# Routing of a graph and expert layer on one core: ScalarE normalises the rows, VectorE takes the low parts, every second block is turned by a transposing DMA

## The reference, cut to what matters

```python
xn = _layernorm(x, axis=-1)
x = x + _L0_gnn_ref(xn, src, dst, edge_weight, W, b) + _L0_mix_ref(xn[None], ...)[0]
x = x + _L0_ffn_ref(_layernorm(x, axis=-1)[None], Wg, bg, W1, b1, W2, b2)[0]
# in _L0_ffn_ref:
gate_scores = einsum('bsd,ed->bse', x, Wg) + bg
topk_scores, topk_idx = top_k(gate_scores, 2)
```

## Time and profile before

| what | value |
|---|---|
| median of 3 runs | 2040.22 us (2038.3 to 2041.55) |
| profiled execution, its own time | 2043.48 us |
| its span (first to last instruction) | 2041.8 us |
| mean granted TensorE clock | 0.945 |
| PE busy | 1662.7 us, 81% |
| DVE busy | 1579.0 us, 77% |
| ACT busy | 1379.6 us, 68% |
| POOL busy | 1247.3 us, 61% |
| DMA traffic | 232.75 MB, mean 114 GB/s |

### The profile page before, as it was taken

How to read it: one execution, slowest core, us unless ns; L and a number is a source line. 1 busy time by engine, 2 the same in 40 slices (tenths; PEclk the granted TensorE clock), 3 DMA queues, 4 the chain that set the end, 5 groups by cost and what they waited for, 6 DMA issues and landing times. The chain is left out here.

```text
span 2041.8 us, 50410 instructions
## 1 busy us (share of the span) xinstructions
PE 1662.7 (81%) x15119; PEld 1287.6 (63%) x15119; DVE 1579.0 (77%) x3370; ACT 1379.6 (68%) x3988; POOL 1247.3 (61%) x1226
## 2 busy tenths in 40 slices
PE   5777668888888788898886666562799999999998
PEld 3455557666666577777764344342677777777776
DVE  8899859898888899989998989887355555555554
ACT  7565458788887778888878878575455555555554
POOL 4357757777777777777777777650344444444443
PEclk7899979999999999999999999855899999999999
DMA  6122355555554544444433346461344444444442
GB/s 223 44 70 80 110 167 157 158 157 159 153 160 151 158 139 124 124 124 121 122 106 101 102 154 185 130 206 26 78 72 73 73 74 71 72 74 71 74 71 43
DMA packets 197501, 232.75 MB, mean 114 GB/s; under 512 B 89207, under 2 KB 154657, under 8 KB 197123
## 3 DMA queue, kind: packets, MB, share of 16 engines
q0 software_dynamic: 62816, 134.68, 25.8%
q1 hardware_dynamic: 128070, 88.47, 15.4%
q10 hardware_dynamic: 6364, 6.40, 0.9%
HBM read 172.28 MB, written 44.36 MB: 106 GB/s over the span
## 5 line engine op out<-in xcount | busy, mean ns | idle before, releaser
L1011 POOL DMA_INDIRECT misc<-z_d,consts x814 | 784.6, 964 | 265.0 <-issue 160.6
L1261 DVE SCALAR_TENSOR_TENSOR acc<-ps,consts,acc 128x512 f32 x814 | 609.2, 748 | 79.3 <-PE ps L1363 60.7
L1034 ACT ACTIVATE misc<-misc 128x256 f16<-128x256 f16 x872 | 391.2, 498 | 74.5 <-DVE misc L1128 69.0
L1891 ACT ACTIVATE misc<-ps,misc 128x128 f32<-128x128 f32 x840 | 240.2, 368 | 276.1 <-PE ps L1851 166.9
L1361 PE MATMUL ps<-misc 128*128 128x256 f16 x1088 | 298.1, 274 | 110.7 <-ACT misc L1034 35.6
L1939 POOL DMA_INDIRECT out<-misc,pos x105 | 166.4, 1585 | 295.5 <-ACT misc L1960 244.7
L1849 PE MATMUL ps<-acc,big 128*128 128x128 f16 x1680 | 328.3, 220 | 14.9 <-DMA acc<-acc 10.0
L1851 PE MATMUL ps<-acc,big 128*128 128x128 f16 x1680 | 330.0, 220 | 0.0
L1850 PE MATMUL ps<-acc,big 128*128 128x128 f16 x1680 | 327.9, 220 | 0.0
L1870 PE MATMUL ps<-big,rec 128*128 x840 | 320.5, 382 | 0.1
L1363 PE MATMUL ps<-misc 128*128 128x256 f16 x1088 | 298.8, 275 | 0.0
(11 more groups left out here) (348 smaller groups left out, 3657.8 us busy)
## 6 DMA issues: line engine op xcount, KB each, us to landing
big<-in_w2T SPq DMA_DIRECT2D x60, 256.0 KB, 2.7
misc<-z_d,consts POOLq DMA_INDIRECT x814
big<-xT_d SPq DMA_DIRECT2D x98, 128.0 KB
big<-in_w1T SPq DMA_DIRECT2D x32, 256.0 KB, 2.8
tok_d<-misc SPq DMA_DIRECT2D x50, 132.0 KB, 1.8
xT_d<-misc SPq DMA_DIRECT2D x49, 128.0 KB
z_d<-misc SPq DMA_DIRECT2D x49, 128.0 KB, 1.7
acc<-in_x SPq DMA_DIRECT2D x6, 896.0 KB
```

Of the source, the lines that this page charges most:

```text
L1011: e.indirect_dma_start(out=rows[n % RB], out_offset=None, in_=c.z_d, in_offset=bass.IndirectOffsetOnAxis(ap=idx[u][:, k:k + 1], axis=0)).t ...
L1034: e.activation(hot[n % HG][:, half, :], same[n % OG], ACT.Copy, scale=near[n // UG % 3][:, t % UG, 1 + half:2 + half]).then_inc(s_hot, 1)
L1261: e.scalar_tensor_tensor(out=rows_of, in0=out_ps[tile % BG], scalar=c.gain, in1=rows_of, op0=ALU.mult, op1=ALU.add).then_inc(s_add, 1)
L1891: l = e.activation(hidden[:, m, :], h_ps[u][:, m, :], ACT.Relu, bias=b1x[u][:, m:m + 1])
```

## The change

What VectorE, ScalarE and GpSimd did for each block is dealt out anew, and one half of the blocks take another way to `xT`:

- `norm` is on ScalarE: one activation (Identity, with a scale and a bias for each partition) writes `xn[i]` in f32, and a second one of the same form, which reads `c.acc3` once more, writes the high part in f16 to `tok[i]`. The bias is -mean times the inverse deviation, one more short operation for each group (`nbias`) on VectorE, behind the reciprocal.
- `lower`, the subtraction of the high part, is on VectorE. GpSimd has nothing left to do in this block but three tables of numbers at its start.
- Blocks with an odd number are turned by a transposing DMA from `tok[i]` to `xT[i]`, issued by SyncE ahead of that block's store. Even blocks are turned by TensorE and copied by ScalarE as before.
- There are four `xn` and four `xT` in place of three and two. `gate(i)` stands two blocks behind `turn` in place of one, and the short operations of `settle` and `invert` and ScalarE's square root stand at other blocks of the group.

```diff
-    XB, TB, GB, LIFT = 3, 6, 7, 2048.0
+    XB, XT, TB, GB, LIFT = 4, 4, 6, 7, 2048.0
+    nbias = more.take(NT)
...
             for i in range(NT):
                 e.wait_ge(s_lo, i + 1)
+                if i % 2 and i >= XT:
+                    e.wait_ge(s_gate, i - XT + 1)
+                if i % 2:
+                    e.dma_start_transpose(xT[i % XT], tok[i % TB][:, 0:2 * D]).then_inc(s_xt[i % XT], 16)
                 e.dma_start(c.tok_d[i * P:i * P + P, :], tok[i % TB].bitcast(F32)).then_inc(s_st[i % TB], 16)
...
-                v.add(e.reciprocal(rstd[:, part], std[:, part]))
-
-            def norm(i):
-                if i >= XB:
-                    e.wait_ge(s_lo, i - XB + 1)
-                e.tensor_scalar(xn[i % XB], c.acc3[:, i:i + 1, :], mean[:, i:i + 1], rstd[:, i:i + 1],
-                                ALU.subtract, ALU.mult).then_inc(s_xn, 1)
+                v.link(e.reciprocal(rstd[:, part], std[:, part]))
+                e.scalar_tensor_tensor(out=nbias[:, part], in0=mean[:, part], scalar=-1.0, in1=rstd[:, part],
+                                       op0=ALU.mult, op1=ALU.mult).then_inc(s_nb, 1)
+
+            def lower(i):
+                e.wait_ge(s_xn, i + 1)
+                e.wait_ge(s_hi, i + 1)
+                e.tensor_tensor(tok[i % TB][:, D:2 * D], xn[i % XB], tok[i % TB][:, 0:D], ALU.subtract).then_inc(s_lo, 1)
...
-            for i in range(NT):
-                e.wait_ge(s_hi, i + 1)
-                e.tensor_tensor(tok[i % TB][:, D:2 * D], xn[i % XB], tok[i % TB][:, 0:D], ALU.subtract).then_inc(s_lo, 1)
...
-                e.copy(tok[i % TB][:, 0:D], xn[i % XB]).then_inc(s_hi, 1)
+                e.activation(xn[i % XB], c.acc3[:, i, :], ACT.Identity, bias=nbias[:, i:i + 1],
+                             scale=rstd[:, i:i + 1]).then_inc(s_xn, 1)
...
+                e.activation(tok[i % TB][:, 0:D], c.acc3[:, i, :], ACT.Identity, bias=nbias[:, i:i + 1],
+                             scale=rstd[:, i:i + 1]).then_inc(s_hi, 1)
...
-                if i >= 2:
+                if i >= 2 and i % 2 == 0:
                     turned_copy(i - 2)
-                if i % GB == (GB - 1 if i < GB else 5) and i < NT - GB:
+                if i % GB == (GB - 1 if i < GB else 4) and i < NT - GB:
                     deviation(i // GB + 1)
...
-            for i in range(NT + 1):
-                if i < NT:
+            for i in range(NT + 2):
+                if i < NT and i % 2 == 0:
                     turn(i)
-                if i >= 1:
-                    gate(i - 1)
+                if i >= 2:
+                    gate(i - 2)
```

More of the change, by code:

```diff
@@ L1422, in route @@
     bg, ones = more.take(NE), more.take(P)
-    XB, TB, GB, LIFT = 3, 6, 7, 2048.0
-    xn = [misc.take(D) for _ in range(XB)]
-    xT = [matrix(misc.take(2 * D, F16), 2 * DH, P) for _ in range(2)]
+    XB, XT, TB, GB, LIFT = 4, 4, 6, 7, 2048.0
+    nbias = more.take(NT)
+    xn = [(misc if k == 0 else more).take(D) for k in range(XB)]
+    xT = [matrix(misc.take(2 * D, F16), 2 * DH, P) for _ in range(XT)]
     tok = [misc.take(ROW, F16) for _ in range(TB)]
@@ L1432, in route @@
     s_blank, s_acc, s_dump = map(S, ("blank", "acc", "dump"))
-    s_w, s_v, s_var, s_std, s_ones, s_xn, s_tr, s_xt, s_gate, s_hi, s_lo = map(S, (
-        "weights", "vector", "var", "std", "ones", "xn", "tr", "xt", "gate", "hi", "lo"))
+    s_w, s_v, s_var, s_std, s_ones, s_xn, s_nb, s_tr, s_copied, s_gate, s_hi, s_lo = map(S, (
+        "weights", "vector", "var", "std", "ones", "xn", "nbias", "tr", "copied", "gate", "hi", "lo"))
+    s_xt = {k: S(f"turned{k}") for k in range(1, XT, 2)}
+    tr_ps = [matrix(c.bank[4 + u][:, 0:D].bitcast(F16), 2 * DH, P) for u in range(2)]
     s_score, s_half, s_wh, s_wl = S("score"), S("half"), S("gate_hi"), S("gate_lo")
     s_st, s_acc0 = [S(f"store{k}") for k in range(TB)], S("acc_first")
-    tr_ps = [matrix(c.bank[4 + u][:, 0:D].bitcast(F16), 2 * DH, P) for u in range(2)]
     g_ps = [matrix(c.bank[u][:, 0:GB * 2 * NE], GB, 2 * NE) for u in range(2)]
@@ L1510, in _ @@
                 g, n = i // GB, i % GB
-                if n == 0:
-                    v.sync()
-                norm(i)
                 if g < NT // GB - 1:
-                    at = n - 1 if g else n - 3
+                    at = n if g else n - 2
                     if 0 <= at < 4:
                         settle(g + 1, at)
-                    if n == GB - 1:
+                    if n == (5 if g else 6):
                         invert(g + 1)
@@ L1524, in _ @@
                         measure(AHEAD + k)
+                lower(i)
             score(NT // GB - 1)
@@ L1548, in rows_out, with norm @@
                             c.acc3[:, g * GB:g * GB + full, :]).then_inc(s_acc0 if g < 3 else s_acc, 16)
-            def high(i):
-                e.wait_ge(s_xn, i + 1)
+            def norm(i):
+                if i % GB == 0:
+                    e.wait_ge(s_nb, i // GB + 1)
+                if i >= XB:
+                    e.wait_ge(s_lo, i - XB + 1)
+                e.activation(xn[i % XB], c.acc3[:, i, :], ACT.Identity, bias=nbias[:, i:i + 1],
+                             scale=rstd[:, i:i + 1]).then_inc(s_xn, 1)
                 if i >= TB:
                     e.wait_ge(s_st[i % TB], 16 * (i // TB))
-                    e.wait_ge(s_tr, i - TB + 1)
-                e.copy(tok[i % TB][:, 0:D], xn[i % XB]).then_inc(s_hi, 1)
+                    if i % 2:
+                        e.wait_ge(s_xt[(i - TB) % XT], 16 * ((i - TB) // XT + 1))
+                    else:
+                        e.wait_ge(s_tr, (i - TB) // 2 + 1)
+                e.activation(tok[i % TB][:, 0:D], c.acc3[:, i, :], ACT.Identity, bias=nbias[:, i:i + 1],
+                             scale=rstd[:, i:i + 1]).then_inc(s_hi, 1)
             def turned_copy(i):
-                e.wait_ge(s_tr, i + 1)
-                if i >= 2:
-                    e.wait_ge(s_gate, i - 1)
-                e.copy(xT[i % 2], tr_ps[i % 2]).then_inc(s_xt, 1)
+                e.wait_ge(s_tr, i // 2 + 1)
+                if i >= XT:
+                    e.wait_ge(s_gate, i - XT + 1)
+                e.copy(xT[i % XT], tr_ps[i // 2 % 2]).then_inc(s_copied, 1)
             EARLY = 4
@@ L1565, in _ @@
             deviation(0)
-            for i in range(NT + 2):
+            for i in range(NT + 3):
                 if i < NT:
-                    high(i)
-                if i >= 2:
+                    norm(i)
+                if i >= 2 and i % 2 == 0:
                     turned_copy(i - 2)
-                if i % GB == (GB - 1 if i < GB else 5) and i < NT - GB:
+                if i % GB == (GB - 1 if i < GB else 4) and i < NT - GB:
                     deviation(i // GB + 1)
@@ L1582, in turn @@
                 e.wait_ge(s_lo, i + 1)
-                if i >= 2:
-                    e.wait_ge(s_xt, i - 1)
+                if i >= 4:
+                    e.wait_ge(s_copied, i // 2 - 1)
                 for h in range(2 * DH):
-                    l = e.transpose(tr_ps[i % 2][:, h, :], tok[i % TB][:, h * P:h * P + P], c.ident16)
+                    l = e.transpose(tr_ps[i // 2 % 2][:, h, :], tok[i % TB][:, h * P:h * P + P], c.ident16)
                 l.then_inc(s_tr, 1)
@@ L1590, in gate @@
                 g, n = i // GB, i % GB
-                e.wait_ge(s_xt, i + 1)
+                if i % 2:
+                    e.wait_ge(s_xt[i % XT], 16 * (i // XT + 1))
+                else:
+                    e.wait_ge(s_copied, i // 2 + 1)
                 if n == 0 and g >= 2:
@@ L1595, in gate @@
                 for h in range(DH):
-                    e.matmul(o, xT[i % 2][:, h, :], wg16[:, h, :], start=h == 0, stop=False)
+                    e.matmul(o, xT[i % XT][:, h, :], wg16[:, h, :], start=h == 0, stop=False)
                 for h in range(DH):
-                    l = e.matmul(o[:, 0:NE], xT[i % 2][:, DH + h, :], wg16[:, h, 0:NE], start=False, stop=h == DH - 1)
+                    l = e.matmul(o[:, 0:NE], xT[i % XT][:, DH + h, :], wg16[:, h, 0:NE], start=False, stop=h == DH - 1)
                 l.then_inc(s_gate, 1)
```

## The result

The changed kernel takes 2055.28 us (median of 5 runs, 2050.47 to 2057.07) against 2040.83 us (5 runs) for the kernel before; the ratio is 1.0066, 95% interval 1.0055 to 1.0077. The medians lie 14.5 us apart where 8.7 were forecast. The direction was right and 2055.3 lies 0.7 us inside the upper end of the range, but outside the 2046 to 2052 us of the forecast's own case: the size was too small.

The account below looks back on a forecast made before the run. VectorE, with ScalarE close behind, was taken to bound most of `route`'s first block. Afterwards ScalarE would bind: +8.2 us to the last copy and 0.5 for the transposing DMA, together +8.7, median 2048.9 us; range 2045 to 2056.

Parts of the forecast that it names:

- the forecast's own case: First block of `route`: ScalarE bound at 0.49 us an activation, transposes hidden; 2046 to 2052 us, chance 0.70.
- What bounds the block, and that it goes into the total in full: First block of `route`: VectorE bounds most of its loop, ScalarE close behind; its gain or loss reaches the total in full.
- The block ends with ScalarE's issues behind the last copy: End of `route`'s first block: ScalarE's last copy plus 4.6 us of DMA issues, which stay.
- ScalarE's price: ScalarE in the loop: 0.49 us an activation, 2.44 us a pair of blocks; last copy 8.2 us later.
- VectorE after: VectorE in the loop: without normalisation but with `lower`, 1.02 us a block at most, below ScalarE's 1.22.
- The transposing DMA: Odd blocks: SyncE's queue keeps up and transposes land within the cover; DMA traffic costs 0.5 us, bounds 0 and 1.0.
- The cover of 4.2 us: Odd blocks: time left for a transpose before ScalarE's copy is held up; it takes 2.65 us, leaving 1.55 us.
- the transpose comes late: Odd blocks: landing doubles to 5.3 us, 2.80 us a pair, +8.6 us on the 8.2, total 2057.0; chance 0.16.
- The signs of being wrong: In the loop: activations under 0.45 us, ScalarE waiting for `lower` in most blocks, or gates waiting for transposes and ScalarE behind.
- The cheap f16 activation: ScalarE's high part: f16 activation as cheap as the cast, 0.31 us; 8.8 us less, 2040.1, no change; chance 0.07.
- the faster case: Loop: VectorE's contention goes and ScalarE doesn't bind; 1.02 us or less a block, 2036.8; chance 0.04.

Follow-up runs that it names:

- with the cast and without the transposes: The change with the high part as a cast of the normalised rows and VectorE copying odd blocks, no transposing DMA: ratio 1.0000, stretch 54.1 us.

## Why the prediction was right, and where it was too small

- *What bounds the block, and that it goes into the total in full*: right. 664.0 to 665.9 us from the next block to the end in every kernel.
- *The block ends with ScalarE's issues behind the last copy*: right, shown by taking three of them out (3.0 and 3.5 us). In the change itself they take 3.76 + 1.51 us against 3.02 + 1.55, 0.7 us that the sum lacked; SyncE was still issuing three stores at that time, which may be why, but no run shows it by itself.
- *ScalarE's price*: right. 591 and 598 ns an activation, start to start 0.49; the kernel without transposes has a stretch of 61.7 us where 1380.3 - 1318.8 = 61.5 were worked out. The f16 output costs nothing and saves nothing. Of the forecast's 8.2 us 0.25 are a later first normalisation (0.2 measured, from the block's first DMA) and 7.9 are stretch, of which that kernel has 8.1.
- *VectorE after*: right that it has room, at most 5.30 of 7 us busy in the windows above.
- *The transposing DMA, forecast at 0.5 us between bounds of 0 and 1.0*: this term was mis-sized. It measured 5.4 us in the stretch. The step that failed is "a pair of blocks costs 1.19 + 2 x 0.32 = 1.83 us of SyncE against 2.44 of the pace", and from it that the queue keeps up. The store's 0.32 us was read where no transpose stood in the queue; two behind one take 1.05 together. A pair costs 2.40 us. Against a pace of 2.44 nothing was left, and each output DMA, behind which a transpose's issue takes 0.8 to 1.4 us longer, puts the queue behind for several pairs. The cover of 4.2 us was reckoned from the issue to the landing, as if the issue came at once; it was the issue that was late. The forecast's landing time of 2.65 us was right (median 2.5).
- *The rival "the transpose comes late"* had the right place and 0.16. Its mechanism, a landing of 5.3 us for all, was only part of it: 7 of the 24 landed 4.1 to 5.0 us after their issue began, most of them because the issue itself was long. Its time, 2057, was nearer the measured 2055.3 than the forecast was. The Trainium skill, "VectorE: DVE Perf Modes", section "The three transpose paths", has 1309 ns a tile; taken four times, the estimate of 5.2 us, it did not hold here either, since four tiles in one DMA land in 2.5 us (median).
- *The signs of being wrong*: one of them came true. TensorE's gates waited for the transposes, 46.1 us in all and over 1 us eleven times from 1350 us on, and ScalarE waited behind them. The last copy started at 1383.2 and the next block at 1389.2 us in an execution whose part in front was 2.65 us shorter, so at 1385.9 and 1391.8 by the prediction's clock. The signs named 1380.5 and 1385.6; by the prediction's own +8.7 they should have been 1380.8 and 1386.0.
- *The cheap f16 activation and the faster case*: out, by 591 ns. But some of the room that the faster case saw was there: with the cast and without the transposes the time is that of before, not less.

What stays open: how the 5.4 us divide between the queue's lateness and slower landings in the bursts. The runs show both (issues of 2.6 us; landings of up to 5.0 us), but taking the output DMAs away, which wins 3.9 us back, removes both at once. So the range held and the direction, for the larger part by ScalarE's price; that a term of 0.5 us where 5.4 were measured did not carry the time out of the range is luck.

## What to carry to other kernels

Price a queue by the rows of the mixture that will stand in it: the issue of a store in a queue of stores says little of one behind a transpose. Add up every engine and every queue per block, not only the one that binds first; here ScalarE (2.44 us a pair) and SyncE's queue (2.40) lay so close that easing ScalarE alone won 0.8 us, and easing both 13.0. And before work is taken off a busy engine, ask what the helper really saves: GpSimd's 33.8 us of subtractions were worth 0.6 us.

## What the runs showed of the hardware

- A store's issue on SyncE's queue takes 0.32 us in a queue of stores; two behind a transposing DMA take 1.05 us together. The transpose's own issue takes 1.20 us, and in the change 2.0 to 2.6 us where ScalarE's queue has just been given an output DMA of 896 KB; in the kernel without these DMAs between the blocks none took over 1.49 us.
- VectorE beside a GpSimd tensor_tensor: a 256-column normalisation takes 0.39 to 0.92 us in the one-input form and 0.46 to 0.93 in the two-input form, and a 7-column operation up to 0.68; with GpSimd idle 0.40 to 0.41 (one input) and at most 0.20.
- Moving 49 stores from SyncE's to GpSimd's queue raised the transposes' median landing from 2.5 to 3.8 us.
